# Second pass over the edges of a graph network: edge activations on two row groups, running sums in two halves

## The chip, the cores and the metric

The kernel runs on one core of one Trainium2 chip. The metric is the device time of one execution in microseconds (us). The profile names the engines of the core PE (TensorE, matmuls; PEld its weight loads), DVE (VectorE), ACT (ScalarE), POOL (GpSimd) and SP (SyncE, which here issues most transfers).

## The reference, cut to what matters

A graph has 3,125 nodes and 103,125 edges, sorted by destination. First an attention block runs over the edges, then five layers of message passing. For this study two parts matter. In the attention block, each edge fetches its source node's row, weighs it for four heads, and all rows of one destination are summed (the 324 columns of a row are 64 for a mean and 4 x 65 for the heads). In the message passing, each layer l needs, per edge, the activation of its 32 attributes:

```
e = leaky(edge_attr @ We1[l] + be1[l])      # slope 0.1; 32 -> 64 columns, l = 0..4
msg = alpha[:, :, None] * h[src]            # four heads
out = segment_sum(msg, dst)                 # sum over the edges of one destination
```

The activations `e` depend on inputs alone, so the kernel computes them long before the layers use them.

## The kernel before, in words

The edges are laid out as 128 partitions of 808 edges each, and worked through in 101 chunks of 8 edges per partition (`K` = 8, `CH` = 101). There are three kinds of pass over the chunks: the first pass (a plain sum over neighbours, and beside it the edge activations of layer 0), the second pass (the attention sums, and beside it the activations of layers 1 to 4), and then one pass for each of the five layers. The change touches the second pass; the first pass shares some of its helpers.

In the second pass the engines work like this, chunk by chunk, each in its own fixed order with semaphores between them:

- POOL (`gather_chunk`, L656) issues eight indirect transfers for a chunk, each fetching one row of 129 values per partition into a ring of four chunks (`SL` = 4). It may fill a place when ACT has copied (`hopcopy`) and DVE has weighed (`msg_steps`) what was in it.
- ACT (`messages`) weighs half of the chunk's rows for the four heads (L824, 16 operations), copies the mean's part (L826, signals `hopcopy`), copies transposed attributes out of PSUM (`copy_attr`, L775), and then runs `leaked` for the next chunk (L785): four activations of 512 columns, each computing 0.1 x (product + bias) for one layer.
- DVE (`gat_chunk`) makes the running sum, eight operations of 324 columns in a chain (L1563), where step k adds row k to step k - 1. Between these it puts four `leaky_edges` (L1364, 512 columns, the max of product + bias and what ACT wrote) at k = 3 to 6, and four `weigh` (L1547, 260 columns) for the next chunk at k = 4 to 7. After each step there is a wait for that step. The next chunk's chain starts when `hopcopy` and the four weighings of it are done.
- PE transposes the attributes of a chunk one ahead (L1009), then runs `first_halves` (L1024): for each of the four layers, two fp32 products with 128 rows, 128 output partitions and 256 columns. The weights in `e1_gat` hold a layer's 32 x 64 matrix four times: product u = 0 has values only in rows 0 to 63, and product u = 1 only in rows 64 to 127; the other half of its rows is zero. Each fp32 product appears in the trace as two MATMUL records and two weight loads. One PSUM bank holds one layer (512 columns), four banks in all, so that a layer's product can be made again when DVE has read that layer of the chunk before.
- SP issues, for chunk c in this order: the load of attributes for chunk c + 3 (L491, L493), four stores of 256 KB of activations of chunk c + 1 (L480), each when its `leaky_edges` is done, and the store of the running sums, 1,296 KB (L542), when all eight steps are done.

Of the kernel before, what the change touches and what calls it, by code (L numbers as in the profile page):

```python
# [19 lines left out]
ACT = mybir.ActivationFunctionType  # L20
# [6 lines left out]
P = 128  # L27
N, F, E, ED = 3125, 64, 103125, 32
H, L = 4, 5
F2 = 2 * F  # L30
K = 8
# [3 lines left out]
CH = T // K  # L35
# [14 lines left out]
LH = 1  # L50
# [8 lines left out]
WG = F + H * WH  # L59
# [37 lines left out]
def build(nc, x, src, dst, attr, W_att, a_src, a_dst, W_g, b_g, W_w, b_w, W1, b1, W2, b2, We1, be1, We2, be2,  # L97
          res_w, dot_scale, ln_g, ln_b, out):
    ctx = ExitStack()
    with ctx:  # L100
# [27 lines left out]
        mask = sb("mask", [P, T])  # L128
# [46 lines left out]
        msg2 = stage[:, 0:2 * K * WG].rearrange("p (b k w) -> p b k w", b=2, k=K)  # L175
        run2 = stage[:, 2 * K * WG:].rearrange("p (b k w) -> p b k w", b=2, k=K)
# [9 lines left out]
        be1_c = sb("be1_c", [P, L])  # L186
# [18 lines left out]
        def part(width):  # L205
# [72 lines left out]
        psum = ctx.enter_context(nc.psum_tensor("psum", [P, 8, 512], F32))  # L278
# [26 lines left out]
        hopcopy, msg_steps, gat_steps = sem("hopcopy"), sem("msg_steps"), sem("gat_steps")  # L305
# [11 lines left out]
        at_ps, at_sb, ya_ps, ya_sb, e_ready, edge_steps = (sem(n) for n in (  # L317
            "at_ps", "at_sb", "ya_ps", "ya_sb", "e_ready", "edge_steps"))
# [51 lines left out]

        def ya(n):

            return psum[:, n % 3 if n < CH * LH else (n - CH * LH) % (L - LH), :]

        def nth(g, i):

            return halves(g - 1) + i
# [29 lines left out]
        def _(sp):  # L407
# [28 lines left out]
            half = ed_edges[0:EP, :].rearrange("(p a t) h -> p a (t h)", p=P, a=2)  # L436
# [99 lines left out]
            for c in range(CH):  # L536
                if c + 3 < CH:
                    load_nat(CH + c + 3)
                if c + 1 < CH:
                    store_acts(CH + c + 1)  # L540
                sp.wait_ge(gat_steps, (c + 3) * K)
                sp.dma_start(chunk_rows(rows2, c, WG), run2[:, c % 2, :, :]).then_inc(rows2_out[c % 2], 16)  # L542

            sp.wait_ge(zero_set, 1)
# [191 lines left out]
        def _(act):  # L736
# [40 lines left out]
            def leaked(g):  # L777

                a, c, _, _, ring, _, l0, layers = pass_of(g)
                for i in range(layers):  # L780
                    act.wait_ge(ya_ps, nth(g, i) + 1)
                    if c >= 2:
                        act.wait_ge(act_out[a][c % 2], 16 * layers * (c // 2))
                        settle()
                    nc.scalar.activation(ring[:, i, :], ya(nth(g, i)), ACT.Identity,  # L785
                                         bias=be_leak[:, l0 + i:l0 + i + 1], scale=LEAK).then_inc(ya_z, 1)

            act.wait_ge(e1_in, 160)
# [27 lines left out]

            def messages(c, s, n):
                act.wait_ge(g2_ready[s], n * (16 * K))
                act.wait_ge(gat_steps, (c + 1) * K)
                settle()  # L820
                for k in range(ON_ACT):
                    for h in range(H):
                        weight = es_w[:, bass.ds(c * K + k, 1), h]
                        nc.scalar.activation(msg2[:, s % 2, k, F + h * WH:F + (h + 1) * WH], gather2[:, s, k, F:W2R],  # L824
                                             ACT.Copy, scale=weight)
                copy(msg2[:, s % 2, :, 0:F], gather2[:, s, :, 0:F]).then_inc(hopcopy, 1)  # L826
                if c + 2 < CH:
                    copy_attr(CH + c + 2)
                if c + 1 < CH:
                    leaked(CH + c + 1)  # L830
# [107 lines left out]
        def _(pe):  # L938
            mm = nc.tensor.matmul
# [26 lines left out]
            for g in range(NG):  # L966
                if g == NG - 1:
                    pe.wait_ge(src_cols_set, 1)
                    for i in range(3):
                        rows = min(P, PE_COLS - i * P)  # L970
                        ins = nc.tensor.transpose(psum[0:rows, 6, i * P:(i + 1) * P], src_cols[:, i * P:i * P + rows], ident[:, :])
# [14 lines left out]
            for a in range(2):  # L986
                ins = mm(psum[:, 0, a * P:(a + 1) * P], ones[:, :], diag[:, a, :], start=True, stop=True)
# [24 lines left out]
            def first_halves(g):  # L1012

                _, _, _, of, _, e1, _, layers = pass_of(g)
                pe.wait_ge(at_sb, g + 1)
                settle()
                for i in range(layers):
                    n = nth(g, i)
                    ahead = 3 if n < CH * LH else L - LH
                    if n >= ahead:  # L1020
                        pe.wait_ge(ya_sb, n - ahead + 1)
                        settle()
                    for u in range(2):
                        ins = mm(ya(n)[:, u * 2 * P:(u + 1) * 2 * P], e1[:, i, u * P:(u + 1) * P], of[:, g % 2, :],  # L1024
                                 start=True, stop=True)
                    ins.then_inc(ya_ps, 1)

            def look_up1(c):

# [52 lines left out]
            for a in range(2):  # L1082
                pe.wait_ge(diag4_ready, a + 1)
                mm(psum[:, a, :], ones[:, :], diag4[:, :, :].rearrange("p h n -> p (h n)"),
                   start=True, stop=True).then_inc(bc4_ready, 1)
# [12 lines left out]
            for c in range(2):  # L1098
                mm(psum[:, 7, c * F:(c + 1) * F], wattT[:, 2 * c:2 * c + 2, :].rearrange("o h i -> o (h i)"), ww_sb[:, 0, :],
                   start=True, stop=True)  # L1100
# [10 lines left out]
            pe.wait_ge(ya_sb, halves(2 * CH - 1))  # L1111
            pe.wait_ge(at_sb, 2 * CH)

            pe.wait_ge(gat_steps, (CH + 2) * K)
            settle()
            pe.wait_ge(fold_sb, 3)
            mm(psum[0:NQ, 7, 0:F], ones[0:1, 0:NQ], fold_b[0:1, :], start=True, stop=True).then_inc(fold_ps, 1)
# [152 lines left out]
        def _(dve):  # L1270
# [88 lines left out]
            def leaky_edges(g, i):  # L1359

                _, _, _, _, ring, _, l0, _ = pass_of(g)
                n = nth(g, i)
                dve.wait_ge(ya_z, n + 1)
                stt(ring[:, i, :], ya(n), be1_c[:, l0 + i:l0 + i + 1], ring[:, i, :],  # L1364
                    ALU.add, ALU.max).then_inc(ya_sb, 1)

            def one_hot1(pair, j0, j1):
# [186 lines left out]
            def gat_chunk(c, s, n1):  # L1554

                s1 = (s + 1) % SL
                dve.wait_ge(hopcopy, c + 1)
                if c >= 2:
                    dve.wait_ge(rows2_out[c % 2], 16 * (c // 2))
                dve.wait_ge(msg_steps, (c + 1) * ON_DVE)  # L1560
                prev = run2[:, (s - 1) % 2, K - 1, :]
                for k in range(K):
                    stt(run2[:, s % 2, k, :], prev, mask[:, bass.ds(c * K + k, 1)], msg2[:, s % 2, k, :],  # L1563
                        ALU.mult, ALU.add).then_inc(gat_steps, 1)
                    prev = run2[:, s % 2, k, :]
                    if c + 1 < CH and 3 <= k < 3 + L - LH:
                        leaky_edges(CH + c + 1, k - 3)
                    if n1 is not None and k >= ON_ACT:
                        if k == ON_ACT:
                            dve.wait_ge(g2_ready[s1], n1 * (16 * K))  # L1570
                        weigh(c + 1, s1, k).then_inc(msg_steps, 1)
                    dve.wait_ge(gat_steps, (c + 2) * K + (k + 1))

            for i in range(L - LH):
                leaky_edges(CH, i)
            dve.sem_inc(gat_steps, 2 * K)
            dve.wait_ge(g2_ready[0], 16 * K)
            for k in range(ON_ACT, K):
                weigh(0, 0, k).then_inc(msg_steps, 1)
# [224 lines left out]
```

## Time and profile before

| | |
|---|---|
| three timed runs, median | 8243.74 us (8239.27 to 8267.42) |
| the profiled execution | 8246.35 us, of which the span shown is 8244.6 us |
| second pass: first to last running-sum step | 1357.0 to 2608.3 us, that is 1251 us, 12.4 us a chunk |
| instructions of L1563 in it | 808, 552 ns each |

The profile's engines are read from the trace of this one execution. "PE psum L1024" is the instruction at line 1024 of the kernel on PE that writes the tensor `psum`. A releaser named after "<-" is what ended an idle time: work on another engine, a DMA, "issue" (the engine waited for nothing that the profile shows) or "remote" (a semaphore that no work in the profile explains at that time).

### The profile page before, as it was taken

To read this page: it belongs to the slowest core of one execution; us is meant where nothing else is said; L and a number is where in the kernel's file an instruction comes from. 1 tells how busy PE (TensorE), PEld (TensorE's weight loads), DVE (VectorE), ACT (ScalarE), POOL (GpSimd) and SP (SyncE) were. 2 spreads that over 40 slices of the span, in tenths; PEclk is the share of its full clock that TensorE was granted. 3 is DMA by queue.
4 is the path that set the end of the run, shared out by engine and by line. 5 is a ranking of instruction groups with operands and counts; after the bars stand their busy time and mean duration, and the time that the engine had idled before them with its cause. 6 is when DMAs were issued, how large, how long until landed. Compare 5 with 4: busy or idle time off the path is not lost.

```text
span 8244.6 us, 120872 instructions
## 1 busy us (share of the span) xinstructions
PE 5713.6 (69%) x44915; PEld 4827.9 (59%) x44915; DVE 5064.5 (61%) x13477; ACT 1731.1 (21%) x3789; POOL 4456.0 (54%) x4429
## 2 busy tenths in 40 slices
PE   5666763445445677776877767787867788687776
PEld 4555552333333566765766766676756676576665
DVE  5555555666676566665666655666646666566665
ACT  1100112555564111111111111111111111111111
POOL 4445557666664455554555545555445555455554
PEclk9777775666677688887888877888868888688887
DMA  3333333777775222322322322233323233133222
GB/s 77 78 78 82 85 86 117 239 238 245 242 255 197 58 77 77 83 76 54 80 77 78 83 62 72 78 82 81 80 51 79 76 84 81 50 79 82 75 77 62
DMA packets 514217, 827.78 MB, mean 100 GB/s; under 512 B 115665, under 2 KB 222042, under 8 KB 500576
## 3 DMA queue, kind: packets, MB, share of 16 engines
q1 hardware_dynamic: 372656, 645.16, 23.1%
q0 software_dynamic: 140976, 174.89, 11.7%
q8 instruction: 359, 5.88, 0.3%
q14 instruction: 226, 1.85, 0.1%
HBM read 385.20 MB, written 434.48 MB: 99 GB/s over the span
## 4 chain that ended last, share of the span: by engine, by line
PE 54%; issue 22%; DVE 11%; another core or an unknown queue 5%; ACT 3%; DMA 2%; SPq 2%; POOL 1%; ACTq 0%; DVEq 0%; POOLq 0%
PE psum L1225 39%; PE psum L1242 7%; PE psum L1037 3%; DVE arena L1563 2%; PE psum L1024 2%; PE psum L1237 2%; DVE arena L1364 2%; ACT arena L824 1%; DVE arena L1373 1%; DMA by_lane<-attr_last 1%; DVE run L1352 1%; POOL agg L663 1%; DVE arena L1628 1%; ACT arena L785 1%
## 5 line engine op out<-in xcount | busy, mean ns | idle before, releaser
L656 POOL DMA_INDIRECT gring<-tableh,src_i x2778 | 2790.4, 1004 | 2492.6 <-DVE psum L1673 1432.0
L1225 PE MATMUL psum<-penalty,arena 125*128 125x192 bf16 x25240 | 2839.4, 263 | 817.2 <-issue 804.6
L1225 PEld LDWEIGHTS psum<-penalty,arena 125*128 125x128 bf16 x25240 | 2304.5, 104 | 1176.9 <-issue 1130.4
L656 POOL DMA_INDIRECT gring<-table,src_i x1414 | 1438.8, 1018 | 1033.1 <-issue 407.7
L1628 DVE TENSOR_SCALAR arena<-dst_f,node_id 125x640 bf16<-125x640 f16 x5060 | 1660.6, 381 | 0.1
L1667 DVE TENSOR_REDUCE gring<-psum 128x128 f32<-128x384 f32 x505 | 330.0, 654 | 1902.0 <-PE psum L1225 1405.6
L889 ACT COPY run<-by_lane 128x512 f32<-128x512 f32 x505 | 571.0, 1131 | 4383.9 <-DVE by_lane L1690 3628.1
L1242 PEld LDWEIGHTS psum<-arena 128*128 128x128 f32 x4040 | 661.3, 229 | 116.3 <-issue 91.5
L1024 PE MATMUL psum<-by_lane,mask_x 128*128 128x256 f32 x1616 | 575.7, 524 | 220.1 <-DVE arena L1364 145.4
L1242 PE MATMUL psum<-arena 128*128 128x128 f32 x4040 | 673.2, 314 | 71.1 <-issue 69.8
L1037 PE MATMUL psum<-x_nodes,arena 125*128 125x204 bf16 x3450 | 465.2, 284 | 258.6 <-issue 221.9
L1690 DVE TENSOR_TENSOR_SCAN by_lane<-mask_x,psum 128x256 f32<-128x256 f32 x1010 | 633.0, 666 | 0.2
L1024 PEld LDWEIGHTS psum<-by_lane,mask_x 128*128 128x128 f32 x1616 | 418.7, 271 | 346.6 <-issue 262.7
L1364 DVE SCALAR_TENSOR_TENSOR arena<-psum,be_c,arena 128x512 f32<-128x512 f32 x505 | 376.7, 746 | 345.4 <-ACT arena L785 234.6
L1037 PEld LDWEIGHTS psum<-x_nodes,arena 125*128 125x128 bf16 x3450 | 349.7, 109 | 368.5 <-issue 345.0
L1563 DVE SCALAR_TENSOR_TENSOR arena<-arena,mask 128x324 f32<-128x324 f32 x808 | 446.2, 552 | 137.8 <-ACT arena L826 69.8
L1225 PE MATMUL psum<-penalty,es_w 125*128 125x192 bf16 x3150 | 425.4, 263 | 105.2 <-issue 104.3
L1225 PE MATMUL psum<-penalty,xin 125*128 125x192 bf16 x3160 | 433.9, 266 | 87.4 <-issue 86.2
L785 ACT ACTIVATE arena<-psum,be_leak 128x512 f32<-128x512 f32 x505 | 333.8, 688 | 577.2 <-remote 302.2
L824 ACT ACTIVATE arena<-gring,es_w 128x65 f32<-128x65 f32 x1616 | 397.7, 343 | 0.3 <-issue 0.3
L1009 PE MATMUL psum<-ident,by_lane 128*128 128x128 f32 x202 | 57.7, 381 | 475.8 <-DMA by_lane<-attr_last 281.7
L1225 PEld LDWEIGHTS psum<-penalty,es_w 125*128 125x128 bf16 x3150 | 293.5, 104 | 149.8 <-issue 145.7
(256 smaller groups left out, 4812.9 us busy)
## 6 DMA issues: line engine op xcount, KB each, us to landing
rows<-arena SPq DMA_DIRECT2D x101, 1296.0 KB
acts<-arena SPq DMA_DIRECT2D x505, 256.0 KB
arena<-acts SPq DMA_DIRECT2D x505, 256.0 KB
rowsg<-run SPq DMA_DIRECT2D x505, 256.0 KB
gring<-tableh,src_i POOLq DMA_INDIRECT x2778
rows<-run SPq DMA_DIRECT2D x101, 256.0 KB
dst_f<-pe_src SPq DMA_DIRECT2D x253, 93.8 KB
gring<-table,src_i POOLq DMA_INDIRECT x1414
```

The lines of the kernel that those rows point to most:

```text
L656: pool.indirect_dma_start(ring[:, s, k, :], None, table, bass.IndirectOffsetOnAxis(ap=src_i[:, c * K + k:c * K + k + 1], axis=0))\
L785: nc.scalar.activation(ring[:, i, :], ya(nth(g, i)), ACT.Identity, bias=be_leak[:, l0 + i:l0 + i + 1], scale=LEAK).then_inc(ya_z, 1)
L824: nc.scalar.activation(msg2[:, s % 2, k, F + h * WH:F + (h + 1) * WH], gather2[:, s, k, F:W2R], ACT.Copy, scale=weight)
L889: copy(run1[:, s, :, :], run_t[:, n % 2, :, :].rearrange("p f k -> p k f")).then_inc(rows_ready, 1)
L1024: ins = mm(ya(n)[:, u * 2 * P:(u + 1) * 2 * P], e1[:, i, u * P:(u + 1) * P], of[:, g % 2, :], start=True, stop=True)
L1037: ins = mm(found1(c)[:, m, :], hot1[c // 2 % 2 * NJ + j][:, at:at + P], parts1[:, j, :, :].rearrange("q a w -> q (a w)"), start=(j == 0), ...
L1225: ins = mm(found(n)[:, m, :], hot_at(n // 2, j)[:, at:at + P], parts[:, j, :, :].rearrange("q a f -> q (a f)"), start=(j == 0), stop=(j == ...
L1242: ins = mm(o, act_in[:, n % SL, at:at + P], cur[:, :], start=False, stop=(u == 3), skip_group_check=True)
L1364: stt(ring[:, i, :], ya(n), be1_c[:, l0 + i:l0 + i + 1], ring[:, i, :], ALU.add, ALU.max).then_inc(ya_sb, 1)
L1563: stt(run2[:, s % 2, k, :], prev, mask[:, bass.ds(c * K + k, 1)], msg2[:, s % 2, k, :], ALU.mult, ALU.add).then_inc(gat_steps, 1)
L1628: ins = ts(hot_at(pair, j), src_row[:, b, :], node_id[:, j:j + 1], None, ALU.is_equal)
L1690: nc.vector.tensor_tensor_scan(run_t[:, b, half, :].rearrange("p f k -> p (f k)"), mask_x[:, b, half, :].rearrange("p f k -> p (f k)"), ms ...
```

## The change

Three edits, all in the second pass.

1. The products for the edge activations use only the 64 rows that are not zero. Product u = 0 reads partitions 0 to 63 and writes one bank, u = 1 reads partitions 64 to 127 and writes the next bank. Layers 0 and 2 of the four lie in banks 0 and 1 (256 columns each), layers 1 and 3 in banks 2 and 3. PE makes layers 0 and 2, signals both, then layers 1 and 3, and signals both. It starts the first pair when DVE has read three layers of the chunk before, and the second when it has read all four. The numbers of matmuls, weight loads and columns stay the same.
2. ACT waits for the pair rather than for one layer, and before the third and fourth activation it also waits until DVE is done with the first and second of the same chunk, since they lie in the same banks. `leaky_edges` moves from k = 3..6 to k = 0..3.
3. Each step of the running sum becomes two operations on columns 0 to 161 and 162 to 323, and each waits for its own half of the step before.

```
 def ya(n):
-    return psum[:, n % 3 if n < CH * LH else (n - CH * LH) % (L - LH), :]
+    if n < CH * LH:
+        return psum[:, n % 3, :].rearrange("p (u n) -> p u n", u=2)
+    i = (n - CH * LH) % (L - LH)
+    return psum[:, i % 2 * 2:i % 2 * 2 + 2, i // 2 * 2 * P:(i // 2 + 1) * 2 * P]
...
 # ACT, leaked
-    act.wait_ge(ya_ps, nth(g, i) + 1)
+    act.wait_ge(ya_ps, nth(g, i) + 1 if a == 0 else nth(g, 0) + 2 * (i % 2 + 1))
+    if i >= 2:
+        act.wait_ge(ya_sb, nth(g, i) - 1)
...
 # PE, first_halves, four layers
+for i in range(2):
+    if g > CH:
+        pe.wait_ge(ya_sb, nth(g, i) - 1)
+        settle()
+    for d in (0, 2):
+        for u in range(2):
+            half = slice(u * F, (u + 1) * F)
+            ins = mm(ya(nth(g, i + d))[:, u, :], e1[half, i + d, u * P:(u + 1) * P], of[half, g % 2, :],
+                     start=True, stop=True)
+    ins.then_inc(ya_ps, 2)
...
 # DVE, gat_chunk
 for k in range(K):
-    stt(run2[:, s % 2, k, :], prev, mask[:, bass.ds(c * K + k, 1)], msg2[:, s % 2, k, :],
-        ALU.mult, ALU.add).then_inc(gat_steps, 1)
+    for d in range(2):
+        part = slice(d * WG // 2, (d + 1) * WG // 2)
+        dve.wait_ge(gat_steps, 2 * ((c + 2) * K + k) - 1 + d)
+        stt(run2[:, s % 2, k, part], prev[:, part], mask[:, bass.ds(c * K + k, 1)], msg2[:, s % 2, k, part],
+            ALU.mult, ALU.add).then_inc(gat_steps, 1)
     prev = run2[:, s % 2, k, :]
-    if c + 1 < CH and 3 <= k < 3 + L - LH:
-        leaky_edges(CH + c + 1, k - 3)
+    if c + 1 < CH and k < L - LH:
+        leaky_edges(CH + c + 1, k)
     if n1 is not None and k >= ON_ACT:
         if k == ON_ACT:
             dve.wait_ge(g2_ready[s1], n1 * (16 * K))
         weigh(c + 1, s1, k).then_inc(msg_steps, 1)
-    dve.wait_ge(gat_steps, (c + 2) * K + (k + 1))
```

The other waits on `gat_steps` count twice as far. In the first pass the same operands are written as two halves of 256 columns that lie side by side.

## Rows read from the trace of the kernel before

**Rows 1.** Waits of all engines in the second pass (1357 to 2615 us): who waited for whom, total us, times, longest.

```profile
PE psum L1009 <- DMA by_lane<-attr_last: 281.7, 67, 6.7
...
ACT arena L785 <- remote: 255.7, 50, 9.1
...
DVE arena L1364 <- ACT arena L785: 199.0, 53, 8.2
POOL gring L656 <- ACT arena L826: 170.3, 24, 10.1
```

**Rows 2.** Groups by line in the second pass (1357 to 2615 us): xcount | busy us, mean ns | idle before.

```profile
L656 POOL DMA_INDIRECT gring<-table,src_i x784 | 811.1, 1035 | 413.7 <-issue 232.0 <-ACT arena L826 170.3 <-DVE arena L1547 6.1
L1024 PE MATMUL psum<-by_lane,mask_x 128*128 128x256 f32 x1584 | 566.3, 525 | 220.1 <-DVE arena L1364 145.4 <-issue 74.6
L1563 DVE SCALAR_TENSOR_TENSOR arena<-arena,mask 128x324 f32<-128x324 f32 x808 | 446.2, 552 | 137.8 <-ACT arena L826 69.8 <-issue 32.3 <-remote 18.3
...
L824 ACT ACTIVATE arena<-gring,es_w 128x65 f32<-128x65 f32 x1600 | 393.7, 344 | 0.0
L1364 DVE SCALAR_TENSOR_TENSOR arena<-psum,be_c,arena 128x512 f32<-128x512 f32 x400 | 298.4, 746 | 295.8 <-ACT arena L785 199.0 <-issue 96.4
L785 ACT ACTIVATE arena<-psum,be_leak 128x512 f32<-128x512 f32 x400 | 261.4, 687 | 490.3 <-remote 255.7 <-PE psum L1024 121.4 <-issue 87.8
L1547 DVE TENSOR_TENSOR arena<-gring,es_w 128x260 f32<-128x260 f32 x400 | 167.6, 419 | 0.0
```

**Rows 3.** Transfers in the second pass (1357 to 2615 us): packets, bytes, mean rate.

```profile
DMA packets 112841, 304.18 MB, mean 242 GB/s; under 512 B 23681, under 2 KB 36097, under 8 KB 99848
```

**Rows 4.** Busy time by stretch, 100 us in the middle of the second pass; x counts instructions.

```profile
core 0: us, PE busy (x) PEld busy (x) DVE busy (x) ACT busy (x) POOL busy (x), PEclk, DMA share, GB/s
2018.00:2043.00 25.00, 13.93 (x45) 11.01 (x46) 23.88 (x48) 20.42 (x64) 19.45 (x18) 0.70 0.87 296
2043.00:2069.00 26.00, 10.66 (x28) 6.56 (x27) 8.44 (x16) 7.96 (x25) 13.81 (x15) 0.63 0.53 178
2069.00:2094.00 25.00, 13.66 (x45) 10.82 (x46) 24.24 (x48) 20.42 (x64) 18.92 (x18) 0.70 0.87 300
2094.00:2118.00 24.00, 9.86 (x29) 6.03 (x27) 9.79 (x19) 10.07 (x30) 15.13 (x16) 0.72 0.64 215
```

**Rows 5.** Timeline of VectorE over one quick chunk: start us, duration us, what.

```profile
2168.14 2.33 DVE L1563 SCALAR_TENSOR_TENSOR arena<-arena,mask 128x324 f32<-128x324 f32 x4 [2.50 <-ACT arena L826]
...
2171.05 0.55 DVE L1563 SCALAR_TENSOR_TENSOR arena<-arena,mask 128x324 f32<-128x324 f32 x1
...
2171.51 0.75 DVE L1364 SCALAR_TENSOR_TENSOR arena<-psum,be_c,arena 128x512 f32<-128x512 f32 x1
...
2172.18 0.42 DVE L1547 TENSOR_TENSOR arena<-gring,es_w 128x260 f32<-128x260 f32 x1
2172.51 0.55 DVE L1563 SCALAR_TENSOR_TENSOR arena<-arena,mask 128x324 f32<-128x324 f32 x1
...
2176.46 2.33 DVE L1563 SCALAR_TENSOR_TENSOR arena<-arena,mask 128x324 f32<-128x324 f32 x4
```

**Rows 6.** Timeline (same columns) of the slow chunk before it, and its products on PE.

```profile
2140.20 3.69 PE L1024 MATMUL psum<-by_lane,mask_x 128*128 128x256 f32 x16
...
2145.46 0.69 ACT L785 ACTIVATE arena<-psum,be_leak 128x512 f32<-128x512 f32 x1 [2.55 <-PE psum L1024]
...
2151.11 0.69 ACT L785 ACTIVATE arena<-psum,be_leak 128x512 f32<-128x512 f32 x1 [4.96 <-PE psum L1024]
...
2158.81 0.69 ACT L785 ACTIVATE arena<-psum,be_leak 128x512 f32<-128x512 f32 x1 [7.02 <-remote]
...
2160.43 2.05 PE L1024 MATMUL psum<-by_lane,mask_x 128*128 128x256 f32 x4 [5.67 <-DVE arena L1364]
...
2163.03 0.69 ACT L785 ACTIVATE arena<-psum,be_leak 128x512 f32<-128x512 f32 x1 [3.52 <-PE psum L1024]
2163.61 3.93 ACT L824 ACTIVATE arena<-gring,es_w 128x65 f32<-128x65 f32 x16
```

More of the change, by code:

```diff
@@ L371, in ya, with in_halves @@
         def ya(n):
-            return psum[:, n % 3 if n < CH * LH else (n - CH * LH) % (L - LH), :]
+            if n < CH * LH:
+                return psum[:, n % 3, :].rearrange("p (u n) -> p u n", u=2)
+            i = (n - CH * LH) % (L - LH)
+            return psum[:, i % 2 * 2:i % 2 * 2 + 2, i // 2 * 2 * P:(i // 2 + 1) * 2 * P]
+        def in_halves(v):
+            return v.rearrange("p (u n) -> p u n", u=2)
         def nth(g, i):
@@ L540, in _ @@
                     store_acts(CH + c + 1)
-                sp.wait_ge(gat_steps, (c + 3) * K)
+                sp.wait_ge(gat_steps, 2 * (c + 3) * K)
                 sp.dma_start(chunk_rows(rows2, c, WG), run2[:, c % 2, :, :]).then_inc(rows2_out[c % 2], 16)
@@ L784, in leaked @@
                         settle()
-                    nc.scalar.activation(ring[:, i, :], ya(nth(g, i)), ACT.Identity,
+                    nc.scalar.activation(in_halves(ring[:, i, :]), ya(nth(g, i)), ACT.Identity,
                                          bias=be_leak[:, l0 + i:l0 + i + 1], scale=LEAK).then_inc(ya_z, 1)
@@ L818, in messages @@
                 act.wait_ge(g2_ready[s], n * (16 * K))
-                act.wait_ge(gat_steps, (c + 1) * K)
+                act.wait_ge(gat_steps, 2 * (c + 1) * K)
                 settle()
@@ L1016, in first_halves @@
                 settle()
[L1017 to L1021, printed above, removed]
+                if layers == 1:
+                    n = nth(g, 0)
+                    if n >= 3:
+                        pe.wait_ge(ya_sb, n - 2)
                         settle()
                     for u in range(2):
-                        ins = mm(ya(n)[:, u * 2 * P:(u + 1) * 2 * P], e1[:, i, u * P:(u + 1) * P], of[:, g % 2, :],
-                                 start=True, stop=True)
+                        ins = mm(ya(n)[:, u, :], e1[:, 0, u * P:(u + 1) * P], of[:, g % 2, :], start=True, stop=True)
                     ins.then_inc(ya_ps, 1)
+                    return
+                for i in range(2):
[8 more added lines that the diff above has]
+                    ins.then_inc(ya_ps, 2)
             def look_up1(c):
@@ L1112, in _ @@
             pe.wait_ge(at_sb, 2 * CH)
-            pe.wait_ge(gat_steps, (CH + 2) * K)
+            pe.wait_ge(gat_steps, 2 * (CH + 2) * K)
             settle()
@@ L1363, in leaky_edges @@
                 dve.wait_ge(ya_z, n + 1)
-                stt(ring[:, i, :], ya(n), be1_c[:, l0 + i:l0 + i + 1], ring[:, i, :],
+                stt(in_halves(ring[:, i, :]), ya(n), be1_c[:, l0 + i:l0 + i + 1], in_halves(ring[:, i, :]),
                     ALU.add, ALU.max).then_inc(ya_sb, 1)
@@ L1571, in gat_chunk @@
                         weigh(c + 1, s1, k).then_inc(msg_steps, 1)
-                    dve.wait_ge(gat_steps, (c + 2) * K + (k + 1))
             for i in range(L - LH):
                 leaky_edges(CH, i)
-            dve.sem_inc(gat_steps, 2 * K)
+            dve.sem_inc(gat_steps, 4 * K)
             dve.wait_ge(g2_ready[0], 16 * K)
```

## The prediction

> **What bounds the kernel now.** All three edits are in the second pass, so I read the profile of that stretch only: 1251 of 8246 us, 101 chunks at 12.4 us. First the waits of all engines [rows 1], to see who is late: nobody waits much for the running sums; DVE waits for ACT's activations (199.0 us), ACT for something marked "remote" (255.7 us), POOL for ACT's copy 24 times (170.3 us), PE for attributes (281.7 us). Then the groups by line [rows 2], for the work of each engine per chunk. POOL: 811.1 us busy and 232.0 us of gaps ("issue") between gathers, (811.1 + 232.0) / 101 = 10.3 us a chunk. DVE: (446.2 + 298.4 + 167.6) / 101 = 9.0 us of durations. ACT about 7.5 us, PE 5.6 us. None is near 12.4 us, so the third view has to show how the chunks are spread in time [rows 4]. A chunk is 16 DVE instructions (8 steps, 4 activations, 4 weighings), and the stretches hold 48, 16, 48 and 19: three chunks in 25 us, then one in 26 us, and so on. The pass runs in cycles of four chunks and some 50 us, about 25 of them, which is also how often POOL waits.
>
> The quick chunks are DVE's: it is busy 23.88 of 25 us, and one chunk takes 2176.46 - 2168.14 = 8.32 us [rows 5]. POOL needs 10.3 us for eight gathers, so it can't follow at that pace; it lives on its ring of four. The transfer queues are close too: shares of 0.87, 0.53, 0.87 and 0.64 over the four stretches [rows 4] make 72.6 us of full queues for eight chunks, 9.1 us a chunk, at 242 GB/s over the pass [rows 3]. In the slow chunk DVE, ACT and POOL all stand, POOL because its ring is full. What ends last there is the activation chain, layer by layer [rows 6]: PE's records put all 16 matmuls of these four products between 2140.20 and 2143.89, but ACT, which waits for them, starts its four activations at 2145.46, 2151.11, 2158.81 and 2163.03. The signals come late, 4 to 8 us after one another; why, the trace doesn't say ("remote"). Once the fourth has come, 2168.14 - 2163.03 = 5.1 us pass to the next chunk's first step: 16 weighings of 3.93 us, the copy, and DVE's chain starts. So there are two prices to work out: a quick chunk (DVE's own time) and the tail of a slow one.
>
> **Running sums in halves.** A step followed by other work costs DVE 2171.51 - 2171.05 = 0.46 us from start to start; an activation 0.67 us, a weighing 0.33 us [rows 5]. The steps that follow each other directly (k = 0 to 2) wait for one another: 2.33 us for four, which is 0.58 us from start to start. In columns, 512 take 746 ns and 324 take 552 ns [rows 2], 1.03 ns a column, so 162 columns fewer save 0.17 us and half a step costs 0.29 us. A pair costs 0.59 us: no more and no less than a waiting step, 0.13 us more than a covered one. Since activations now lie at k = 0 to 3 and weighings at 4 to 7, no half waits for its own predecessor: it ended at least one operation earlier. The quick chunk is then 4 x (0.59 + 0.67) + 4 x (0.59 + 0.33) + 0.2 (from the last weighing to the next chunk, as now) = 8.9 us against 8.3: +0.6 us.
>
> The trace shows no operation of 162 columns, so the bounds. Below: the fixed part of the weighing, 0.33 us less 260 columns at 1.03 ns = 0.06, gives 0.23 for a half and 0.46 for a pair, and a chunk of 7.9 us (-0.4). Above: if each half waits out its predecessor, 0.385 us of duration and 0.03 us of gap, a pair is 0.83 us and a chunk 10.8 us (+2.5). I take 0.29, since it stands on the same operation.
> Of fixed cost per instruction the rows say 0.46 us less 324 columns at 1.03 ns, that is 0.13 us. The Trainium skill (VectorE: DVE Perf Modes, "The TRN2 errata") says the same kind of thing, that many small tiles pay a latency per instruction which one large tile pays once, and speaks against halves; its table has 58 cycles at 0.96 GHz (0.06 us) from SBUF to SBUF. By that figure a pair would be 0.46 us and the chunk a gain of 0.4 us; by the rows it is a loss of 0.6 us.
>
> **Activations at k = 0 to 3.** In a slow chunk this decides. Now, after the last product is noticed, DVE has only one activation, two weighings and a step left, and ACT's 5.1 us are longer. Afterwards products come in pairs, (0, 2) and then (1, 3), and the last signal is the one for layer 1, which stands at k = 1. Behind it are queued: ACT's second activation to DVE's start, 0.72 us (2159.53 - 2158.81, as now), DVE 0.67, a pair 0.59, 0.67, 0.59, 0.67, then four pairs with weighings 4 x 0.92 = 3.7, and 0.2: 7.8 us, +2.7 us. ACT's own way is shorter: 0.72, DVE's 0.75 for layer 1, for which ACT's fourth activation now waits, and then the 5.1 us as before: 6.6 us, +1.5 us. POOL's ring is freed by ACT's copy, so POOL stands 1.5 us longer.
>
> **Row groups.** Same matmuls, weight loads and columns. If the two row groups work side by side, PE's 5.6 us a chunk fall towards 2.8. In quick chunks PE isn't waited for, so it is worth nothing; SP's order is unchanged and its stores of activations go 2 us earlier in the chunk, with the transfer queues as full as before. In the slow chunk the price of the late signals is what counts, and I can't say from the trace whether it hangs on PE's work: four MATMUL records take 2.05 us there at half clock [rows 6], but 4 to 8 us go by. I keep them at their length. A new cover that is needed: PE may begin the next chunk only after DVE's third activation (3.8 us into the chunk) instead of its first, and must have the first pair ready 8.9 us into it. Transposes and one pair at half clock without any overlap are 0.7 + 4.1 us, so the first pair is in time; the second (another 4.1 us) only if row groups overlap.
>
> **The sum.** Per cycle of four chunks: three quick ones +1.8 us, the slow one +2.7 us: 4.5 us x 25 = +113 us if nothing absorbs it. But quick chunks of 8.9 us still outrun POOL's 10.3, and what they lose leaves POOL's ring fuller; what surely lengthens the cycle is POOL's longer stand, 1.5 us x 25 = +38 us. I take +65 us, nearer to the lower, because the gathers need 41 of the 50 us of a cycle. Against the profiled execution 8246.35 + 65 = 8311 us; the median of the runs is 2.6 us lower, so 8310 us is forecast.
>
> **Rivals.**
> *A, faster: late signals shrink with PE's work.* If row groups side by side also halve the 4 to 8 us between products, the slow chunk loses about 9 of its 26 us. POOL then bounds: 101 x 10.3 = 1040 us and a short stand per cycle, say 1100 to 1140 us for the pass, -110 to -150 us: about 8115 us. The limit of this is 1040 us, 8035 us. For it: ACT's and DVE's idle time in slow chunks are these signals and nothing else [rows 1, 6]. Against it: they are two to three times longer than the array work between them. It decides once the gaps fall below 3.5 us. The Trainium skill (TensorE: Matmul & The Clock Gate, Part 3) says that matmuls in different row groups run concurrently, with 3.07x measured for four of them; that would make PE's part so short, but it says nothing of the signals.
> *B, no change: everything is absorbed.* Slower quick chunks keep the ring fuller, the transfer queues get slack (9.1 of 8.9 us), and the slow chunk starts later or ends sooner by as much: 8246 us.
> *C, the row groups don't overlap.* Then at half clock the second pair is ready 3.8 + 0.7 + 8.2 = 12.7 us into a chunk, where it is wanted at about 10.0: quick chunks of 11.6 us, above POOL's 10.3. 75 x 2.7 = 200 us: about 8450 us. Against it: the clock is at full speed nearly half of the time (0.63 to 0.72 in the stretches [rows 4]), and half a product has no rows in common with the other.
>
> **Chances and range.** Forecast (slower by 40 to 115 us) 0.48, A 0.29, B 0.15, C 0.08. A measurement of this kernel can tell about 0.3% (25 us) from no change. So faster 0.29, same 0.15, slower 0.56. The range goes from 8110 us, in the middle of A, to 8400 us, which leaves out C and the upper bound of the half step; below 8110 lie some 0.13, above 8400 some 0.07. Without A and C the forecast's own range is 8284 to 8360 us.
>
> **What would show it.** L1563's group should have 1616 operations near 385 ns; starts of two halves 0.29 us apart; a quick chunk 8.9 us; between ACT's second activation of a slow chunk and the next chunk's first step 7.8 us; four chunks in 51 to 54 us. PE MATMUL records in the pass should be as many as before, their joint busy time about half. The prediction is wrong if the slow chunks vanish or shorten (A), if a half starts 0.23 or 0.41 us after the other, or if DVE waits at its second activation in quick chunks too (C).

## The result, and the profile after

The changed kernel takes 8372.6 us (median of 4 runs, 8335.7 to 8395.6), the kernel before 8255.6 us (4 runs) beside it: a ratio of 1.0127, 95% interval 1.0094 to 1.0161 (the ratio comes from runs side by side; the two medians are 117 us apart). The profiled execution took 8362.3 us. Its second pass goes from 1351.2 to 2742.6 us, 1391 us instead of 1251: the pass grew by 140 us and the rest shrank by 24, as much as executions differ.

Groups by line in the second pass of the changed kernel, which answer to [rows 2] (L1042 are the products, L1584 the running sums, L1382 `leaky_edges`, L794 `leaked`, L663 the gathers):

```profile
L663 POOL DMA_INDIRECT gring<-table,src_i x785 | 776.8, 990 | 572.7 <-DVE arena L1565 325.0 <-issue 239.1 <-remote 6.8
L1584 DVE SCALAR_TENSOR_TENSOR arena<-arena,mask 128x162 f32<-128x162 f32 x1616 | 545.8, 379 | 37.0 <-remote 15.1 <-issue 11.1 <-DVE arena L1565 10.8
...
L1042 PE MATMUL psum<-by_lane,mask_x 64*128 64x256 f32 x1584 | 367.6, 640 | 347.6 <-DVE arena L1382 330.6 <-issue 17.0
L1382 DVE SCALAR_TENSOR_TENSOR arena<-psum,be_c,arena 128x512 f32<-128x512 f32 x400 | 298.0, 745 | 459.1 <-ACT arena L794 309.5 <-issue 149.7
L794 ACT ACTIVATE arena<-psum,be_leak 128x512 f32<-128x512 f32 x400 | 263.8, 685 | 660.3 <-remote 504.6 <-issue 114.3 <-DVE arena L1382 21.4
```

The running sums are 1,616 operations of 379 ns (forecast: 385). The products are as many as before; each record is longer (640 against 525 ns, at a mean granted clock of 0.56 in the pass against 0.69), but they lie side by side: 367.6 us busy against 566.3 [rows 2]. So the row groups do overlap. Yet three waits have grown: ACT for "remote" 504.6 us against 255.7, DVE for ACT 309.5 against 199.0 and POOL 325.0 (for the weighings) against 170.3 [rows 1].

VectorE over a quick chunk, which answers to [rows 5]:

```profile
2010.04 0.68 DVE L1584 SCALAR_TENSOR_TENSOR arena<-arena,mask 128x162 f32<-128x162 f32 x2 [0.20 <-DVE arena L1565]
2010.64 0.74 DVE L1382 SCALAR_TENSOR_TENSOR arena<-psum,be_c,arena 128x512 f32<-128x512 f32 x1
2011.30 0.68 DVE L1584 SCALAR_TENSOR_TENSOR arena<-arena,mask 128x162 f32<-128x162 f32 x2
2011.89 0.74 DVE L1382 SCALAR_TENSOR_TENSOR arena<-psum,be_c,arena 128x512 f32<-128x512 f32 x1
...
2019.09 0.69 DVE L1584 SCALAR_TENSOR_TENSOR arena<-arena,mask 128x162 f32<-128x162 f32 x2 [0.20 <-issue]
...
2022.78 0.75 DVE L1382 SCALAR_TENSOR_TENSOR arena<-psum,be_c,arena 128x512 f32<-128x512 f32 x1 [1.76 <-ACT arena L794]
```

A pair takes 0.60 us from start to start (forecast 0.59), and the chunk 2019.09 - 2010.04 = 9.05 us (forecast 8.9). In it DVE starts its second activation (2011.89) without a wait; in the next chunk it waits 1.76 us there. Of the 70 chunks of under 15 us, 25 have such a wait of over 0.5 us, 61 us in all; the kernel before has none. The slow chunk of the same cycle, which answers to [rows 6]:

```profile
2025.66 3.78 PE L1042 MATMUL psum<-by_lane,mask_x 64*128 64x256 f32 x16
...
2029.98 0.69 DVE L1584 SCALAR_TENSOR_TENSOR arena<-arena,mask 128x162 f32<-128x162 f32 x2 [0.20 <-DVE arena L1565]
...
2036.91 0.69 ACT L794 ACTIVATE arena<-psum,be_leak 128x512 f32<-128x512 f32 x1 [7.68 <-remote]
...
2046.05 1.26 ACT L794 ACTIVATE arena<-psum,be_leak 128x512 f32<-128x512 f32 x2 [8.46 <-remote]
...
2053.97 0.68 DVE L1584 SCALAR_TENSOR_TENSOR arena<-arena,mask 128x162 f32<-128x162 f32 x2 [0.20 <-DVE arena L1565]
```

PE's records put all products between 2025.66 and 2029.44, but the first pair is noticed at 2036.91 and the second at 2046.05. From ACT's second activation to the next chunk it is 2053.97 - 2046.05 = 7.9 us (forecast 7.8), and 7.9 is also the middle value of all 30 slow chunks. Three chunks by stretch, which answer to [rows 4]:

```profile
2010.04:2019.09 9.05, 3.12 (x14) 2.38 (x16) 8.85 (x25) 6.40 (x22) 5.40 (x6) 0.50 0.90 314
2019.09:2029.98 10.89, 5.62 (x24) 3.25 (x22) 8.93 (x25) 6.95 (x22) 8.45 (x9) 0.66 0.85 280
2029.98:2053.97 23.99, 4.45 (x18) 3.06 (x18) 9.02 (x24) 8.29 (x24) 9.43 (x10) 0.50 0.43 135
```

The cycle is now mostly three chunks long. Over the pass, 30 chunks are slow (over 15 us, 22.6 us on average); before it were 27 of 22.2 us. Of the pass's 140 us, 78 lie in the slow chunks and 62 in the others.

A count that the rest of the text uses: how often ACT waits over 3.5 us before an activation of L794 (L785 before), by its own records, whatever the releaser named. I call it a **late signal**. Before there are 62, 342 us in all; after, 64 with 485 us: +143 us, beside the pass's +140 us. The count takes long waits, whatever made them long. In the changed kernel PE's last record of such a product ended 1.9 to 22.5 us before each of the 64, 9.4 us in the middle; in the kernel before 14 of 62 come within 1.5 us of one.

Which signal is late changes too. Before, 59 of the 62 waits stand before the second, third or fourth activation of a chunk. After, 25 stand before the first activation, for the first pair, and 39 before the second, for the second pair. Before the first one ACT has another reason to wait: the stores of the activations of two chunks earlier must be done (`act_out`), of which nothing is said above. The traces exclude the moving of these bytes: the last of the 512 packets of 2,048 bytes that make up those stores had ended at least 12.9 us before each late first signal, in every kernel below. Before the later activations of a chunk that wait is already over.

### The profile page after: what moved, and what is told of

It is laid out like the page before. It is cut to its first block, busy times and chain, and to the rows that moved or that the text cites. A ratio compares the mean times of both kernels' runs of the same rounds, so it can differ in the third digit from the quotient of the medians.

```text
span 8360.6 us, 121677 instructions
## 1 busy us (share of the span) xinstructions
PE 5531.4 (66%) x44915; PEld 4684.4 (56%) x44915; DVE 5143.4 (62%) x14285; ACT 1733.6 (21%) x3789; POOL 4421.5 (53%) x4429
## 4 chain that ended last, share of the span: by engine, by line
PE 53%; issue 21%; DVE 10%; another core or an unknown queue 7%; ACT 4%; POOL 1%; DMA 1%; SPq 1%; ACTq 0%; DVEq 0%; POOLq 0%
PE psum L1243 39%; PE psum L1260 7%; PE psum L1055 3%; ACT arena L833 2%; DVE arena L1584 2%; DVE arena L1382 2%; PE psum L1255 2%; DVE arena L1391 1%; POOL agg L670 1%; DVE run L1370 1%; ACT arena L794 1%; DVE arena L1565 1%; PE psum L1202 1%; PE psum L1032 0%
## 5 line engine op out<-in xcount | busy, mean ns | idle before, releaser
L663 POOL DMA_INDIRECT gring<-tableh,src_i x2778 | 2788.8, 1004 | 2474.8 <-DVE psum L1693 1415.7
L663 POOL DMA_INDIRECT gring<-table,src_i x1414 | 1404.7, 993 | 1188.3 <-issue 414.3
L1382 DVE SCALAR_TENSOR_TENSOR arena<-psum,be_c,arena 128x512 f32<-128x512 f32 x505 | 376.0, 745 | 511.8 <-ACT arena L794 348.5
L1042 PE MATMUL psum<-by_lane,mask_x 64*128 64x256 f32 x1616 | 373.5, 637 | 349.3 <-DVE arena L1382 332.3
L1584 DVE SCALAR_TENSOR_TENSOR arena<-arena,mask 128x162 f32<-128x162 f32 x1616 | 545.8, 379 | 37.0 <-remote 15.1
L1042 PEld LDWEIGHTS psum<-by_lane,mask_x 64*128 64x128 f32 x1616 | 262.8, 324 | 429.5 <-issue 384.4
L794 ACT ACTIVATE arena<-psum,be_leak 128x512 f32<-128x512 f32 x505 | 336.0, 685 | 739.2 <-remote 548.4
L1018 PEld LDWEIGHTS psum<-ident,by_lane 128*128 128x128 f32 x202 | 29.1, 203 | 730.9 <-issue 730.9
```

Of the source, the lines that this page charges most:

```text
L663: pool.indirect_dma_start(ring[:, s, k, :], None, table, bass.IndirectOffsetOnAxis(ap=src_i[:, c * K + k:c * K + k + 1], axis=0))\
L794: nc.scalar.activation(in_halves(ring[:, i, :]), ya(nth(g, i)), ACT.Identity, bias=be_leak[:, l0 + i:l0 + i + 1], scale=LEAK).then_inc(ya_ ...
L1042: ins = mm(ya(nth(g, i + d))[:, u, :], e1[half, i + d, u * P:(u + 1) * P], of[half, g % 2, :], start=True, stop=True)
L1382: stt(in_halves(ring[:, i, :]), ya(n), be1_c[:, l0 + i:l0 + i + 1], in_halves(ring[:, i, :]), ALU.add, ALU.max).then_inc(ya_sb, 1)
L1584: stt(run2[:, s % 2, k, part], prev[:, part], mask[:, bass.ds(c * K + k, 1)], msg2[:, s % 2, k, part], ALU.mult, ALU.add).then_inc(gat_ste ...
```

## The experiments

Prices below are ratio less 1, times 8250 us.

**Which edit costs: one alone, two alone, one undone.**

*Halves only*, in the kernel before:

```
+for d in range(2):
+    part = slice(d * WG // 2, (d + 1) * WG // 2)
+    dve.wait_ge(gat_steps, 2 * ((c + 2) * K + k) - 1 + d)
+    stt(run2[:, s % 2, k, part], prev[:, part], ...)
```

> The kernel before with edit 3 alone: each step of the running sum in two halves, activations still at k = 3 to 6, products and their waits as before. Two theories. T, prices of VectorE: the time of the change is made of a quick chunk (8.3 us before, 9.0 after) and of the tail of a slow chunk, in cycles of four chunks as before. R, run-ahead of TensorE: it is made of the products coming in pairs and starting only after the third activation, so that late signals hit every third chunk instead of every fourth. T expects a quick chunk of 8.9 us and some 40 to 60 us more than before (about half of the change's +110). R expects the quick chunk of 8.9 us too, but cycles of four chunks, and at most 20 us more than before, since gathers need 10.3 us a chunk anyway.

Measured: 8282.6 us, ratio 1.0050 (1.0027 to 1.0073): +41 us. Quick chunks 9.05 us, cycles of three chunks, and 65 late signals with 418 us. Theory T holds in size, but not in form: the three-chunk cycle was in neither expectation for this run, and it is the changed kernel's. The trace has 33 slow chunks instead of 27, 681 us in them instead of 601, while the others sum to 609 us instead of 646.

*The changed kernel with whole steps:*

```
-    for d in range(2):
-        (two operations of 162 columns)
+    stt(run2[:, s % 2, k, :], prev, ...)   # k = 0..3 still carry leaky_edges
```

> The changed kernel with whole steps of 324 columns again (edits 1 and 2 without edit 3). A quick chunk should be 4 x (0.46 + 0.67) + 4 x (0.46 + 0.33) + 0.2 = 7.9 us by the rows of before, 1.1 us less than in the changed kernel. T expects 60 to 90 us less than the changed kernel, about the time of before or 30 us above. R expects at most 20 us less than the changed kernel: 90 to 120 us above before, with slow chunks as often as in the changed kernel (one in three).

Measured: 8287.1 us, ratio 1.0051 (1.0018 to 1.0083). Next to the changed kernel's 1.0127 the halves cost +63 us; R falls.

*Row groups only:* whole steps, and `leaky_edges` at k = 3..6 as before.

```
-    if c + 1 < CH and k < L - LH:
-        leaky_edges(CH + c + 1, k)
+    if c + 1 < CH and 3 <= k < 3 + L - LH:
+        leaky_edges(CH + c + 1, k - 3)
```

> Row groups and pairs with whole steps, and the activations at k = 3 to 6 again. Tail of a slow chunk: after the last product are left two activations, steps and weighings from k = 4, so T expects it about 1 us shorter than with activations at k = 0 to 3 and the pass the same or faster than in e2_whole_steps by 20 to 30 us. R expects TensorE to start still later in the chunk (after k = 5 instead of k = 2), less run-ahead, and a time at or above that of e2_whole_steps, up to 60 us more.

Measured: 8182.9 us, ratio 0.9922 (0.9894 to 0.9951): 64 us faster than before. T had the direction (faster than with whole steps), but by 20 to 30 us and not by 106; R had it the other way. The slow chunks fell to 16.8 us and there are 36 late signals with 278 us, 1.1 for a slow chunk instead of 2.3; 34 of them are of the second pair and 2 of the first. Its waits in the second pass, next to [rows 1]:

```profile
ACT arena L794 <- remote: 254.9, 41, 15.2
...
DVE arena L1382 <- ACT arena L794: 120.2, 21, 8.0
```

*The move only:* the kernel before with `leaky_edges` at k = 0..3 (`k < L - LH`) and nothing else.

> The kernel before with the activations at k = 0 to 3 and nothing else. No step follows another directly at k = 0 to 3, so a quick chunk is 7.9 us instead of 8.3. T expects 20 to 30 us less than before. R expects no change within 20 us, cycles of four chunks, since the gathers' 10.3 us a chunk and the late signals set the cycle.

Measured: 8244.9 us, ratio 1.0013 (0.9985 to 1.0040). No difference; T's gain of 20 to 30 us lies outside the interval.

*The changed kernel without the move:* the same diff as for row groups only, with the halves kept.

> The changed kernel with its activations back at k = 3 to 6 (row groups and halves stay). Theory M, prices add up: the move costs what it cost with whole steps (8287 less 8183, 104 us), so 8372 - 104 = about 8268 us; slow chunks near 17 us again, quick chunks near 9.9 us. Theory H, the halves cost little when no pair of them lies behind the last activation that the next chunk waits for, as in the kernel before (32 us): 8183 + 32 = about 8215 us, quick chunks 9.4 to 9.6 us. If it is above 8300 us, the move is not the costly edit and both theories fall.

Measured: 8247.1 us, ratio 0.9953 (0.9924 to 0.9981). The kernel before took 8277.0 us beside it, so only the ratio can be set against the expectations: against 8250 us it is 8211, near theory H's 8215 and below M's 8268. The halves cost 26 us here. Undoing this one edit of the three turns 1.3% slower into 0.5% faster, 144 us. Late signals: 35 with 284 us.

**What in the row groups helps.** *Pairs, but all rows:*

```
-    ins = mm(ya(nth(g, i + d))[:, u, :], e1[half, i + d, ...], of[half, g % 2, :], ...)
+    ins = mm(ya(nth(g, i + d))[:, u, :], e1[:, i + d, ...], of[:, g % 2, :], ...)
```

> The faster kernel (row groups, whole steps, activations at k = 3 to 6; 8183 us) but every product again over all 128 rows: same pairs, same banks, same signals, only no side-by-side work. Theory O, the gain comes from the overlap on the array, which shortens the late signals: slow chunks 22 us or more, quick chunks 10 us or more since the second pair comes late, time 8250 us or more. Theory S, it comes from the signals in pairs and from the later start of the products (after three activations instead of one): slow chunks stay near 17 us and the time within 25 us of 8183.

Measured: 8234.8 us, ratio 0.9943 (0.9915 to 0.9971), slow chunks 17.2 us, 37 late signals with 282 us. Theory S fits by the ratio (17 us from row groups only; the kernel before took 8277.0 us beside it): most of the gain comes without any overlap. The 17 us are within the intervals, some 25 us to either side of each price. What remains is signals and banks in pairs together with the later start of the products; no run takes these apart. PE shows it in the stretch from 1400 to 2500 us, row groups only first, all rows second; neither PE's busy time (402.79 and 556.66 us) nor its mean granted clock (0.58 and 0.72) moves the slow chunks:

```profile
1400.00:2500.00 1100.00, 402.79 (x1680) 273.53 (x1676) 758.08 (x1495) 670.41 (x2052) 770.28 (x749) 0.58 0.78 259
```

```profile
1400.00:2500.00 1100.00, 556.66 (x1654) 418.17 (x1654) 749.27 (x1475) 665.85 (x2023) 756.66 (x736) 0.72 0.76 254
```

*One step later:* row groups only, with `leaky_edges` at k = 4..7 (`4 <= k < 4 + L - LH`).

> The faster kernel (row groups, whole steps) with the activations one step later, at k = 4 to 7. Theory T, the tail behind the last signal decides: one step less of it, 0.5 to 0.9 us in each of some 33 slow chunks, 8155 to 8170 us. Rival, the quick chunks decide: the products start one step later (0.6 us), DVE waits that much longer for the first one, 66 x 0.4 to 0.6 us = 26 to 40 us more, 8210 to 8225 us.

Measured: 8240.8 us, ratio 0.9948 (0.9919 to 0.9978). The rival: quick chunks grew from 9.3 to 10.3 us (middle values), while the slow ones fell from 33 to 18. It is 21 us slower than row groups only, with intervals that overlap, and k = 3..6 stays the best place found.

**What the late signals depend on.** The next four runs found the machine otherwise: the kernel before took 6035.2 us (26 runs, 6023 to 6042) on the same chip that had given 8250.6 us 38 minutes earlier, and ratios are against that. There is no trace of the kernel before in this condition; the run with products twice has to stand for it.

*Products twice:*

```
-    for u in range(2):
+    for u in (0, 1, 0, 1):      # second pass only
```

> The kernel before, with each product of the second pass made twice (same result). It tells on what the late signals depend. Theory I, each TensorE instruction takes some 0.70 us to be reported in those stretches, so a layer's signal comes after eight of them (5.6 us) now: with 16 instructions a layer the signals of a slow chunk come about 11 us apart, a slow chunk grows from 22 to 40 us or more and the second pass by 400 us or more. Theory A, array work counts: it doubles from 5.6 to 11.2 us a chunk, which still fits under the 12.4 us; every chunk becomes 11 to 13 us, the slow chunks grow by a few us, the pass by 50 to 200 us. Theory Q, the lateness is a delay of the signal alone (a full queue somewhere): slow chunks stay within 3 us.

Measured: 6031.9 us, ratio 0.9999 (0.9990 to 1.0008). No chunk is over 15 us and there is no late signal. The busy parts are those of before: running sums of 557 ns (552), gathers of 1042 (1035). What differs is who waits for whom; here the second pass (1010 to 2075 us) of this kernel:

```profile
DVE arena L1547 <- DMA gring<-table,src_i: 159.6, 85, 3.0
ACT arena L824 <- DMA gring<-table,src_i: 142.0, 74, 3.7
```

DVE and ACT now wait for rows to be gathered. In the five layer passes, whose code is the same, DVE's reading of PE's products waits 1902 us in the kernel before at 8246 us, and 49 us here:

```profile
L1667 DVE TENSOR_REDUCE gring<-psum 128x128 f32<-128x384 f32 x505 | 330.0, 654 | 1902.0 <-PE psum L1225 1405.6 <-remote 496.2
```

```profile
L1667 DVE TENSOR_REDUCE gring<-psum 128x128 f32<-128x384 f32 x505 | 325.3, 644 | 49.1 <-PE psum L1225 48.5 <-issue 0.6
```

*Half the instructions:* one product of 2 x 256 columns for a layer; the second product is left out, and its half of the values repeats the first.

```
-    for u in range(2):
-        ins = mm(ya(n)[:, u * 2 * P:(u + 1) * 2 * P], e1[:, i, u * P:(u + 1) * P], of[:, g % 2, :], ...)
+    ins = mm(ya(n).rearrange("p (u n) -> p u n", u=2), e1[:, i, 0:P],
+             of[:, g % 2:g % 2 + 1, :].broadcast_to([P, 2, 2 * P]), ...)
```

> The kernel before, with one product of 2 x 256 columns for a layer instead of two of 256: same columns, half the matmuls and half the weight loads. The second half then repeats the first (half of the edge activations of layers 1 to 4 have wrong values). Theory I (0.70 us for each instruction): signals 2.8 us apart instead of 5.6, slow chunks near 12 to 14 us, the pass at 1090 to 1150 us and the kernel at 8100 to 8150 us, faster than with row groups. Theory A (array work counts): the columns are the same, slow chunks stay above 19 us and the time within 40 us of the kernel before. Theory Q: no change either.

Measured: 6034.2 us, ratio 0.9998 (0.9989 to 1.0007). No late signal.

*No activation stores:* in the second pass they are left out, and the layers read those of layer 0.

```
-    sp.dma_start(acts[l0 + i, c, :, :], ring[:, i, :]).then_inc(act_out[a][c % 2], 16)
+    sp.sem_inc(act_out[a][c % 2], 16)                    # second pass
-    sp.dma_start(act_in[:, s, :], acts[l, c, :, :])...
+    sp.dma_start(act_in[:, s, :], acts[0, c, :, :])...
```

> The kernel before without the stores of edge activations in the second pass (1 of 3 MB a chunk; the layers read those of layer 0 instead, as many bytes). If full transfer queues bring on the late signals: DMA share below 0.6, few or no remote waits on ACT (255.7 us before), chunks near 10.3 us (POOL's gathers), the pass at 1050 to 1100 us, the kernel 150 us or more faster. If unbroken gathers of POOL or the number of TensorE instructions bring them on: still slow chunks above 18 us in cycles of three or four, the remote waits above 150 us, and the kernel within 60 us of before.

Measured: 6022.3 us, ratio 0.9977 (0.9967 to 0.9987). The DMA share of the second pass is 0.58 instead of 0.85 and it gives 13 us over the whole kernel. No late signal. These three were to tell what makes the signals late; there was nothing late to explain, so they say only that without late signals the products are not on the path, and these stores hardly.

*Halves and the move*, without row groups: halves only, with `leaky_edges` at k = 0..3.

> The kernel before with two of the three edits: halves, and activations at k = 0 to 3; no row groups. It is the last of the eight combinations. If the move costs only together with the pairs (the last signal then stands at k = 1, with two late signals ahead of it): as halves alone, 1.003 to 1.007 of before. If halves and the move are costly together whatever the products do: 1.010 or more.

Measured: 5990.6 us (5 runs), ratio 0.9924 (0.9911 to 0.9938). Neither expectation had a gain; both were made for the slower condition, in which this kernel was not run.

*The changed kernel again*, unchanged, on another chip on which the kernel before took 6035.4 us:

> The changed kernel once more, unchanged, beside the kernel before, since in the last set of runs the kernel before itself took 6035 us, its second pass 1064 to 1071 us, with no late signals at all. If it is again so: theory L, the change costs time only through the late signals of TensorE: without them POOL's gathers bound the pass (8 x 1.3 = 10.3 us, above the 9.0 us of a quick chunk), so the changed kernel is not slower, 0.990 to 1.000 of the kernel before, as halves with the move were (0.992), and the second pass near 1030 us. Theory D, DVE's 0.7 us more per chunk count in themselves: 1.005 or more, the second pass 1100 us or more. If the kernel before takes about 8250 us again, the ratio is 1.010 to 1.016 as measured first.

Measured: 5989.3 us, ratio 0.9921 (0.9907 to 0.9934). Theory L: in the condition without late signals the change makes the kernel 46 us faster. Its second pass lasts 1030 us (1064 in the kernel with products twice), with chunks of 9.0 to 12 us:

```profile
L663 POOL DMA_INDIRECT gring<-table,src_i x784 | 778.3, 993 | 239.0 <-issue 226.2 <-DVE arena L1565 12.8
L1584 DVE SCALAR_TENSOR_TENSOR arena<-arena,mask 128x162 f32<-128x162 f32 x1614 | 549.5, 384 | 100.8 <-ACT arena L835 99.3 <-DVE arena L1565 1.4
L1042 PE MATMUL psum<-by_lane,mask_x 64*128 64x256 f32 x1584 | 357.7, 626 | 9.2 <-DVE arena L1382 9.2
L1382 DVE SCALAR_TENSOR_TENSOR arena<-psum,be_c,arena 128x512 f32<-128x512 f32 x400 | 298.9, 747 | 15.1 <-ACT arena L794 11.9
```

POOL is the bound: (778.3 + 239.0) / 101 = 10.1 us a chunk, of 10.2. DVE costs the same as in the slower runs (L1584 at 384 against 379 ns), but it waits for ACT for 11.9 us instead of 309.5. The granted clock isn't the difference: this pass runs at a mean of 0.62 with no late signal, that of the kernel before at 0.69 with 62.

The late signals in the second pass, by kernel, from the trace of each:

| kernel | late signals | us in them | slow chunks | pass, us |
|---|---|---|---|---|
| before | 62 | 342 | 27 | 1251 |
| halves only | 65 | 418 | 33 | 1294 |
| move only | 62 | 381 | 31 | 1283 |
| changed, whole steps | 53 | 414 | 26 | 1289 |
| changed | 64 | 485 | 30 | 1391 |
| row groups only | 36 | 278 | 33 | 1189 |
| changed, without the move | 35 | 284 | 32 | 1207 |
| pairs, all rows | 37 | 282 | 32 | 1204 |
| one step later | 37 | 243 | 18 | 1223 |
| halves and move; changed again (at 6035 us) | 0 | 0 | 0 | 1031; 1030 |

## Why the forecast held, and what in it did not

Forecast were 8310 us, slower by 65 us; measured is slower by 105 us (78 to 133 by the interval). It lies within the range, and the sign was right, as were two of the prices: the quick chunk's work and the tail behind the last signal. That the total fits is in part luck: the first edit gained what was held to be nothing, the move cost more, and it came through late signals, which the forecast had kept as they were. Point by point:

- **Price of a half step: right.** 0.30 us from start to start against 0.29, and 9.05 us for the quick chunk against 8.9. By the fixed part in the table of the Trainium skill (VectorE: DVE Perf Modes, "The TRN2 errata"; the same section says that the row comes out too low for a single operation) a pair would take 0.46 us, an estimate, and the chunk would gain; the trace disagrees with that figure, a pair takes 0.60 us. Its rule that many small tiles pay a latency each holds here: two halves last 2 x 379 ns, the whole step 552.
- **Halves in the sum: right in size, by luck.** 75 x 0.6 = 45 us of a chunk's lengthening; halves alone cost 41 us. But in their trace it is more slow chunks that cost (33 instead of 27), not longer quick ones, as said there. In the full change it is 63.
- **The tail behind the second signal: right, but the slow chunk isn't.** The tail is 7.9 us against 7.8. The slow chunk as a whole was to grow by 2.7 us and grew by 0.4 on average; instead there are three more of them.
- **"I keep them at their length": wrong, and it is the step that failed.** I held the late signals to be untouched by the first edit and priced it at nothing. Alone it is worth -64 us, and with `leaky_edges` at k = 3..6 only 1.1 signals a slow chunk are late instead of 2.3. Nor was rival A right about the reason: with all rows, and so no overlap, the slow chunks are as short.
- **The move: mis-sized.** Priced at 25 x 1.5 to 2.7 us, 38 to 67 us. By itself it costs nothing that can be measured (+11 us, -12 to +33); on top of the pairs 106 us, on top of pairs and halves 144 us. With it there is a second late signal in a slow chunk (2.1 against 1.1), that of the first pair: 25 in the changed kernel and 18 with whole steps, against 2 to 6 in the kernels with pairs and the activations at k = 3 or later. (The move alone does this as well, 16 instead of 3, but there the later layers' signals are late less often, and the count stays at 62.) Each long wait is 7.6 us on average, against 5.5 in the kernel before, where a signal is of one layer. The tail that I worked out is a part of it only.
- **The choice between 38 and 113 us: too low.** I took 65 because the gathers would absorb some. The upper sum of 113 us is near what came, but it came about as -64 + 106 + 63 = 105, not by the terms of the sum.
- **Four chunks in 51 to 54 us: wrong in form.** There are mostly three chunks in a cycle of 44 us. Halves alone do this (9, 9, 21).
- **Rival C's reason fell, its sign came in part:** the joint busy time of the products fell to 0.65 of before (forecast: about half), so the row groups do overlap. But in 25 of the 70 quicker chunks DVE does wait at its second activation, 61 us in all, which the forecast had at nothing. In the condition without late signals no chunk has such a wait of over 0.5 us, so PE's work isn't the reason.

Shown is which edits cost in the slower condition, and that the change's sign hangs on that condition: it costs 1.3% where signals are late and gains 0.8% where none is, with the same durations of DVE's operations and of the gathers. Over the kernels above, the time in late signals and the pass always move the same way, but not by the same amount: +143 and +140 us for the change, -64 and -62 for row groups only, but +76 and +43 for halves only, +72 and +38 for whole steps, -99 and -28 for "one step later". So the count tells the direction and is no price. Shown is as well that neither PE's busy time nor its mean granted clock sets the length of the slow chunks. Not shown is why signals are late, nor why the move makes a chunk's first signal late, nor whether pairs or the later start of the products shorten the slow chunks. The three runs made for the first of these met a machine without late signals.

The gain without late signals was in none of my sums. Halves with the move have it (0.9924), and row groups add nothing to it (0.9921). The gathers have become shorter: 993 ns against 1042 in the kernel with products twice, 784 x 0.05 = 38 us, and the pass is 34 us shorter. By the records, 109 of 784 gathers take over 1.1 us against 215 of 781. Which of the two edits does it was not tried in this condition. In the slower one the gathers take 998 ns with halves only and 1028 with the move only, which points to the halves, but 1030 in the changed kernel without the move. By what they are shortened, no run shows.

## What to carry to other kernels

Before you price an edit at a stall that the trace can't explain ("remote", or a signal long after the work's record), ask what the edit does to the number of such signals on the path; here an edit that was priced at nothing was worth 64 us. Try each part of a change alone and also each undone: three edits of -64, +11 and +41 us made +105 together, and in the slower condition the best version was one of the three alone (in the other it was not run). And measure the kernel before beside every run, also in a second session: the change has the other sign there.

## What the runs showed of the hardware that was not expected

- The same kernel on the same chip took 8250.6 us and, 38 minutes later, 6035.2 us. Durations of operations are nearly alike (the products of L1225 are 263 and 247 ns in their traces, at a mean granted clock of 0.81 and 0.94 in the layer passes); what is gone are waits for PE, 1902 against 49 us for DVE's L1667 alone, where the layer passes are some 1,700 us shorter. In these passes (2700 to 7900 us) 404 of 34,790 neighbouring weight loads start 0.68 to 0.72 us apart in the kernel before; in the run with products twice (2200 to 5900 us) 3 of 35,964 do. What puts the machine in either condition, nothing here shows.
- The trace itself differs between the conditions. All nine traces of the slower condition hold 37,000 to 39,000 semaphore updates, all five of the other 117,000 to 124,000, with about as many instructions. Of the 3,264 landings of one semaphore of the activation stores, the kernel before has 792 on record and products twice 3,252. So in the slower condition a releaser "remote", or a wait put down to a DMA, can be a record that is missing; the waits themselves are from each engine's own records.
- In the slower condition PE's record of a product can end 16.6 us before the waiting engine is let go (2029.44 and 2046.05 above), where that engine has nothing else left to wait for. The Trainium skill (Perfetto Trace Analysis, "Tensor Engine Instruction (MATMUL, LD_WEIGHTS)") says that the end of a TensorE record is estimated from the instruction's size. The trace agrees in so far as these ends don't tell when the signal comes; whether it is the work or the signal that is late, no run here shows.
- Products of 64 rows on two row groups take 640 ns each instead of 525 (mean granted clock 0.56 and 0.69), and the joint busy time falls from 566 to 368 us, 0.65 and not one half.
- Indirect gathers take 990 to 998 ns on average in four of the five kernels with halves, and 1022 to 1048 ns in the fifth and in the nine without.
